# Turning activations to channels: f16 parts with tokens on the partitions, or f32 transposes with a split behind

## What is computed

```python
h = embed(x) * sqrt(192) + position
u = rmsnorm(layernorm(h)) * norm1_w
z, xBC, dt = split(u @ in_proj_w)            # 192 -> 384 + 512 + 24
y = scan(silu(conv4(xBC)), softplus(dt + bias)) * silu(z)
m = y @ out_proj_w
v = rmsnorm(m) * norm2_w
h = h + m + (silu(v @ w_gate) * (v @ w_up)) @ w_down   # MLP of 768
x = layernorm(h)
s = sigmoid(x @ gate_weight.T)               # 8 experts, 2 chosen of 2 groups of 4
out = h + shared_expert(x) + sum_of_chosen_experts(x)  # 9 pairs w1/w3 of 128, w2
```

## Time and profile before

| what | us |
|---|---|
| median of 3 runs | 852.89 (852.64 to 852.89) |
| the profiled execution | 854.33 |
| its span, first to last instruction | 852.5 |
| PE busy | 794.0 (93%) |
| DVE busy | 656.8 (77%) |
| ACT busy | 540.8 (63%) |
| POOL busy | 294.4 (35%) |
| mean granted PE clock | 0.986 of full speed |

### The profile page before, as it was taken

The page is one execution under the profiler, slowest core; times in us unless marked ns, Lnnn a source line. Parts: engine busy times, 40 slices in busy tenths (PEclk is TensorE's granted clock), DMA queues, the critical chain, the costliest instruction groups (busy, mean ns, idle before and its releaser), DMA issues.

```text
span 852.5 us, 23075 instructions
## 1 busy us (share of the span) xinstructions
PE 794.0 (93%) x7310; PEld 657.5 (77%) x7310; DVE 656.8 (77%) x1680; ACT 540.8 (63%) x1208; POOL 294.4 (35%) x445
## 2 busy tenths in 40 slices
PE   3567999999999999999999999999999999999897
PEld 2345787878888887888888787888878788887786
DVE  5785987977778797777879777787978778787645
ACT  4735576766667676666767676675767767576533
POOL 2552242343324234332423434242343424233222
PEclk9788999999999999999999999999999999999999
DMA  7600000000000000010000000000000000000000
GB/s 259 173 2 14 1 7 19 5 20 0 23 0 5 17 3 20 0 23 0 5 17 4 19 0 23 0 5 17 5 18 0 23 0 5 17 5 10 2 1 20
DMA packets 17107, 16.77 MB, mean 20 GB/s; under 512 B 6322, under 2 KB 15416, under 8 KB 16824
## 3 DMA queue, kind: packets, MB, share of 16 engines
q1 hardware_dynamic: 17080, 16.43, 6.8%
HBM read 12.23 MB, written 4.19 MB: 19 GB/s over the span
## 4 chain that ended last, share of the span: by engine, by line
PE 81%; DVE 6%; issue 5%; DMA 3%; ACT 3%; POOL 1%; SPq 1%; ACTq 0%; DVEq 0%; POOLq 0%
PE bank L1462 37%; PE bank L1743 7%; PE bank L1630 7%; PE bank L1812 6%; PE bank L1619 6%; PE bank L1712 4%; PE bank L1699 3%; PE bank L1690 3%; PE bank L1675 3%; DMA wt_raw<-weights 2%; DVE xa L1057 2%; PE bank L1468 2%; PE bank L1560 1%; PE bank L1470 1%; ACT L725 1%
## 5 line engine op out<-in xcount | busy, mean ns | idle before, releaser
L1114 DVE SCALAR_TENSOR_TENSOR mr<-er,gm 128x512 f32<-128x512 f32 x192 | 136.8, 735 | 29.1 <-ACT er L743 27.7
L743 ACT ACTIVATE er<-bank 128x512 f32<-128x512 f32 x192 | 109.5, 597 | 52.1 <-PE bank L1619 47.3
L1812 PE MATMUL bank<-w2t,w_raw 128*128 128x192 f32 x576 | 112.4, 326 | 0.0
L1057 DVE SCALAR_TENSOR_TENSOR xa<-xr,cw_,xa 128x256 f32<-128x256 f32 x192 | 92.9, 493 | 9.3 <-ACT xa L663 7.3
L814 ACT ACTIVATE sg<-bank 128x256 f32<-128x256 f32 x144 | 55.1, 383 | 59.3 <-PE bank L1462 48.2
L1812 PEld LDWEIGHTS bank<-w2t,w_raw 128*128 128x128 f32 x576 | 91.0, 190 | 1.3
L774 ACT ACTIVATE sg<-bank 128x256 f32<-128x256 f32 x90 | 34.6, 384 | 89.2 <-PE bank L1462 89.2
L1283 DVE TENSOR_TENSOR w_raw<-sg,bank 128x256 f32<-128x256 f32 x144 | 60.2, 418 | 37.3 <-ACT sg L814 36.1
L1462 PE MATMUL bank<-x_h,w_hi 128*128 128x256 f16 x288 | 78.3, 272 | 4.1 <-DVE w_raw L1283 3.9
L1630 PE MATMUL bank<-mr,xd 128*32 128x128 f32 x1536 | 69.4, 286 | 12.3 <-DVE mr L1114 12.1
L1462 PE MATMUL bank<-x_h,wt_lo 128*128 128x256 f16 x288 | 78.5, 273 | 0.0
(11 more groups left out here) (240 smaller groups left out, 2144.6 us busy)
## 6 DMA issues: line engine op xcount, KB each, us to landing
out<-w_raw SPq DMA_DIRECT2D x16, 192.0 KB, 2.0
w_raw<-weights SPq DMA_DIRECT2D x1, 1924.0 KB, 9.8
wt_raw<-weights SPq DMA_DIRECT2D x2, 962.0 KB, 15.6
pos<-position SPq DMA_DIRECT2D x16, 96.0 KB, 2.8
ri<-exponent_rows SPq DMA_DIRECT2D x4, 384.0 KB, 4.0
tok<-tokens SPq DMA_DIRECT2D x16, 70.0 KB
sums<-lj SPq DMA_DIRECT2D x16, 64.0 KB, 2.2
ri<-sums SPq DMA_DIRECT2D x64, 12.0 KB
```

Of the source, the lines that this page charges most:

```text
L743: act.activation(er[:, r % NER], p_d[r % 2][:].rearrange("p (h i) -> p h i", h=HG), ACT.Exp)\
L1057: ve.scalar_tensor_tensor(xa[:, m], xr[:, m, :, k:k + Q], cw_[:, m, k:k + 1], xa[:, m], ALU.mult, ALU.add)\
L1114: ve.scalar_tensor_tensor(mr[:, r % NER], er[:, r % NER], 1.0, gm[:, r // NQ, :].unsqueeze(1).to_broadcast([128, HG, Q]), ALU.min, ALU.mult)\
L1812: ins = pe.matmul(p_ex[e][:, b * D:(b + 1) * D], hh[:, e % NHH, b * Q:(b + 1) * Q], w2t[:, e, :], start=True, stop=True)
```

## The change

Each value is split while tokens are still on the partitions, and the f16 parts are turned.

- `u_t`, `v_t` and `x_t` hold for each channel the high and the low f16 part side by side (`[128, NB, D, 2]`). The high part: for u a new ACT step `pre_high` (two scalings of `uc`), for v `mixed_norm` with another destination, for x two DVE multiplications of `xc`. The low part: a new DVE step `low_parts`, two operations (source times scale minus high part).
- For u and x the mean is subtracted first, by two more DVE operations right behind the statistics (`uc`, `xc`).
- PE's `turn` does six f16 products with an f16 identity in place of four f32 transposes: two with the high parts of channels 0 to 127 (every second element of `u_t` as weights) after a wait for the high part; then, after a wait for the low part, two with both parts of channels 128 to 191 interleaved, and two with the low parts of channels 0 to 127, into another bank.
- Behind it ACT copies the bank to f16 in one operation of 512 elements (`high_in`), and DVE copies the low half in one of 256 (`low_in`).
- The tail's rows are now repeated one by one (c, c, c+1, c+1, ...) and not as a block; the host lays them out, and `wt_raw` comes in one DMA of 128 rows for each part.
- Order: v's turn moves behind the fifth `masked` and the eighth `exponents`; DVE's `v_low` stands between masks 4 and 5; `pre_low` stands behind the fourth gate product, ACT's `pre_high` behind the fourth `silu`; x's subtraction stands ahead of `steps_dt`, and its low part right behind its high part, ahead of masks 10 and 11. In the ramp `set_skip` moves behind the first split, an f16 identity is made by ACT, and DVE's weight split is in two steps.

The diff, cut to its core (ACT and the loads; then DVE; then PE and the host):

```diff
-                sp.dma_start(wt_raw[0:DT, part], weights[DH:D, part]).then_inc(in_w, 16)
-                sp.dma_start(wt_raw[DT:128, part], weights[DH:D, part]).then_inc(in_w, 16)
+                sp.dma_start(wt_raw[:, part], weights[DH:DH + 128, part]).then_inc(in_w, 16)
                 sp.dma_start(nrm[:], norms).then_inc(in_w, 16)
 
...
-            act.wait_ge(in_w, 64)
+            act.wait_ge(in_first, 48)
+            act.copy(id16[:], idf[:]).then_inc(setup_a, 1)
+            act.wait_ge(in_w, 48)
...
-            act.wait_ge(in_first, 48)
-            for k in range(KT):
-                act.activation(skip[:, k], idf[:], ACT.Copy, scale=dsk[:, k:k + 1]).then_inc(setup_a, 1)
-
-            def split(c, done, src, hi, taken, head, tail):
-
-                act.wait_ge(done, c + 1)
+
+            def set_skip():
+                for k in range(KT):
+                    act.activation(skip[:, k], idf[:], ACT.Copy, scale=dsk[:, k:k + 1]).then_inc(setup_a, 1)
+
+            def high_in(c, turned, src, hi, taken, ready):
+
+                act.wait_ge(turned, c + 1)
                 if later(c):
                     act.wait_ge(taken[0], c * taken[1])
-                act.copy(hi[:, 0, :], src[:, 0:NB * Q]).then_inc(head, 1)
-                act.copy(hi[DT:128, 1, :], src[DT:128, NB * Q:2 * NB * Q]).then_inc(tail, 1)
+                act.copy(hi[:], src[:].rearrange("p (k t) -> p k t", k=2)).then_inc(ready, 1)
 
...
             def mixed_norm(c, src=p_out[0]):
                 act.wait_ge(rm_ready, c + 1)
                 if later(c):
-                    act.wait_ge(vt_done, c)
+                    act.wait_ge(vl_turned, c)
                 for b in range(NB):
-                    ins = act.activation(vn[:, b, :], src[:, b * D:(b + 1) * D], ACT.Copy, scale=rm[:, b:b + 1])
-                ins.then_inc(vn_ready, 1)
+                    ins = act.activation(v_t[:, b, :, 0], src[:, b * D:(b + 1) * D], ACT.Copy, scale=rm[:, b:b + 1])
+                ins.then_inc(vh_ready, 1)
...
                     act.activation(sg[:, f % 2, :], p_pair[f % 2][:, 0:NB * Q], ACT.Silu).then_inc(sg_ready, 1)
+                    if f == 3 and p is not None:
+                        pre_high(p)
                     if f == 4 and p is not None:
                         pre_split(p)
...
+            def pre_high(c):
+                act.wait_ge(uc_ready, c + 1)
+                act.wait_ge(r0_ready, c + 1)
+                if later(c):
+                    act.wait_ge(ul_turned, c)
+                for b in range(NB):
+                    ins = act.activation(u_t[:, b, :, 0], uc[:, b, :], ACT.Copy, scale=r0[:, b:b + 1])
+                ins.then_inc(uh_ready, 1)
+
             def pre_split(c, src=p_misc):
-                split(c, ut_done, src, u_h, (z_done[0], 1), u_hi_ready, u_hi_tail)
+                high_in(c, uh_turned, src, u_h, (z_done[0], 1), u_hi_ready)
...
             def ramp():
+                pre_high(0)
                 pre_split(0)
+                set_skip()
                 softplus(0)
-                for i in range(2):
-                    convolved_in(0, i, p_d)
-                    first_tap(0, i)
+                convolved_in(0, 0, p_d)
+                first_tap(0, 0)
+                pre_high(1)
+                convolved_in(0, 1, p_d)
+                first_tap(0, 1)
                 gates(0, 1)
                 gates(0, 0)
                 pre_split(1, p_out[1])
```

```diff
-            def split(c, head, tail, src, hi, lo, lo_ready, lo_tail):
-
-
-                ve.wait_ge(head, c + 1)
-                ve.wait_ge(tail, c + 1)
-                ve.tensor_tensor(lo[:], src[:, 0:NB * Q], hi[:, 0, :], ALU.subtract).then_inc(lo_ready, 1)
-                ve.tensor_tensor(hi[0:DT, 1, :], src[DT:128, NB * Q:2 * NB * Q], hi[DT:128, 1, :], ALU.subtract)\
-                    .then_inc(lo_tail, 1)
+            def low_parts(c, src, scale, parts, ready):
+
+                for b in range(NB):
+                    ins = ve.scalar_tensor_tensor(parts[:, b, :, 1], src[b], scale[:, b:b + 1], parts[:, b, :, 0],
+                                                  ALU.mult, ALU.subtract)
+                ins.then_inc(ready, 1)
+
+            def low_in(c, turned, src, lo, ready):
+                ve.wait_ge(turned, c + 1)
+                ve.tensor_copy(lo[:], src).then_inc(ready, 1)
...
                 ve.wait_ge(h0_ready, c + 1)
+                if later(c):
+                    ve.wait_ge(uh_ready, c)
+                    ve.wait_ge(ul_ready, c)
...
                 ve.bn_aggr(mv[:, 1, :], stat[:, 1, :]).then_inc(stat_ready, 1)
-
-            def pre_apply(c):
+                ve.wait_ge(stat_ready, c + 1)
+                for b in range(NB):
+                    ins = ve.tensor_scalar(uc[:, b, :], h0_next[:, b, :], mv[:, b, 0:1], None, ALU.subtract)
+                ins.then_inc(uc_ready, 1)
+
+            def pre_low(c):
+                ve.wait_ge(uc_ready, c + 1)
                 ve.wait_ge(r0_ready, c + 1)
-                if later(c):
-                    ve.wait_ge(ut_done, c)
-                ve.tensor_scalar(un[:, 0, :], h0_next[:, 0, :], mv[:, 0, 0:1], r0[:, 0:1], ALU.subtract, ALU.mult)
-                ve.tensor_scalar(un[:, 1, :], h0_next[:, 1, :], mv[:, 1, 0:1], r0[:, 1:2], ALU.subtract, ALU.mult)\
-                    .then_inc(un_ready, 1)
-
-            def pre_split(c, src=p_misc):
-                split(c, u_hi_ready, u_hi_tail, src, u_h, u_l, u_lo_ready, u_lo_tail)
+                ve.wait_ge(uh_ready, c + 1)
+                low_parts(c, (uc[:, 0, :], uc[:, 1, :]), r0, u_t, ul_ready)
+
+            def pre_split(c, src=p_out[1][:, NB * Q:2 * NB * Q]):
+                low_in(c, ul_turned, src, u_l, u_lo_ready)
...
+                    if p is not None and t == 3:
+                        pre_low(p)
                     if f is not None and t in (0, 3):
                         masks(f, (6 + t // 3,))
                     if p is not None:
                         if t == 1:
                             pre_add(p)
                             pre_stats(p)
-                        if t == 2:
-                            pre_apply(p)
                         if t == 4:
                             pre_split(p)
...
                 ve.bn_aggr(mv2[:, 1, :], stat2[:, 1, :]).then_inc(stat2_ready, 1)
+                ve.wait_ge(stat2_ready, c + 1)
+                for b in range(NB):
+                    ins = ve.tensor_scalar(xc[:, b, :], h1[:, b, :], mv2[:, b, 0:1], None, ALU.subtract)
+                ins.then_inc(xc_ready, 1)
...
             def norm2_apply(c):
                 ve.wait_ge(r2_ready, c + 1)
-                if later(c):
-                    ve.wait_ge(xnt_done, c)
+                ve.wait_ge(xc_ready, c + 1)
+                if later(c):
+                    ve.wait_ge(xl_turned, c)
                 for b in range(NB):
-                    ins = ve.tensor_scalar(xn[:, b, :], h1[:, b, :], mv2[:, b, 0:1], r2[:, b:b + 1], ALU.subtract, ALU.mult)
-                ins.then_inc(xn_ready, 1)
+                    ins = ve.tensor_scalar(x_t[:, b, :, 0], xc[:, b, :], r2[:, b:b + 1], None, ALU.mult)
+                ins.then_inc(xh_ready, 1)
+                ve.wait_ge(xh_ready, c + 1)
+                low_parts(c, (xc[:, 0, :], xc[:, 1, :]), r2, x_t, xl_ready)
...
+            def v_low(c, src=p_out[0]):
+                ve.wait_ge(vh_ready, c + 1)
+                low_parts(c, (src[:, 0:D], src[:, D:2 * D]), rm, v_t, vl_ready)
+
             def split_v(b):
-                split(b, v_hi_ready, v_hi_tail, p_out[1], v_h, v_l, v_lo_ready, v_lo_tail)
+                low_in(b, vl_turned, p_pair[1][:, 0:NB * Q], v_l, v_lo_ready)
 
             def split_x(b):
-                split(b, x_hi_ready, x_hi_tail, p_out[1], x_h, x_l, x_lo_ready, x_lo_tail)
+                low_in(b, xl_turned, p_out[0][:, NB * Q:2 * NB * Q], x_l, x_lo_ready)
...
                 if f is not None:
                     masks(f, range(4))
                     from_state(f, 0)
-                    masks(f, (4, 5))
+                    masks(f, (4,))
+                v_low(b)
+                if f is not None:
+                    masks(f, (5,))
                 split_v(b)
                 mixed(b)
```

```diff
-            def transpose_channels(dst, src, done):
-
+            def turn(c, dst, low, parts, high_ready, low_ready, high_turned, low_turned):
+
+                pe.wait_ge(high_ready, c + 1)
                 for b in range(NB):
-                    pe.transpose(dst[:, b * Q:(b + 1) * Q], src[:, b, 0:DH], idf[:])
+                    pe.matmul(dst[:, b * Q:(b + 1) * Q], parts[:, b, 0:DH, 0], id16[:], start=True, stop=True)
+                pe.wait_ge(low_ready, c + 1)
                 for b in range(NB):
-                    ins = pe.transpose(dst[:, (NB + b) * Q:(NB + b + 1) * Q], src[:, b, D - 128:D], idf[:])
-                ins.then_inc(done, 1)
```

(37 more changed lines are left out.)

98 lines of the change are left out of this document (49 added, 49 removed).

## The result

The changed kernel takes 865.48 us (median of four runs, 864.00 to 866.65) against 852.76 before: a ratio of 1.0142, 95% interval 1.0122 to 1.0161. The forecast was 872.8. The profiled execution took 866.65 us with a span of 864.9.

What follows compares the result with a forecast made beforehand. TensorE, busy 93% of the span, was taken as the bound; 1.15 + 0.30 - 0.10 = 1.35 us per body, times 14 = 18.9, plus 1.0 finale, gave 19.9 and a median of 872.8 us, range 857 to 885.

Steps and rivals of the forecast that it cites:

- the waits ahead of the third product: Sign at x's and u's turns: TensorE idles until VectorE's low part, near 1.0 us per chunk for x with mask 9.
- masks 8 and 9 later: Sign on VectorE at x: masks 8 and 9 begin 0.7 us later behind the statistics.
- v's turn without its wait for ScalarE: Sign on TensorE: v's turn, now behind the fifth masked group, shows no wait for ScalarE's high part.
- x, 1.15 forecast: Term at x's turn: VectorE's added subtractions and low parts delay TensorE, costing 1.15 us per chunk.
- u, 0.30 forecast: Term at u's turn: ScalarE's high parts, then VectorE's low parts, cost 0.30 us per chunk, bounds 0.05 and 0.65.
- v, -0.10 forecast: Term at v's turn: a gain of 0.14 us per chunk, of which 0.10 was kept, bounds -0.2 and +0.2.
- The ramp, 0 forecast: Term before the loop: the wait for the wt_raw load covers the added operations, 0 us, bounds -1 and +1.
- The finale, +1.0 forecast: Term after the loop: chunk 14's v and x turns in the same surroundings cost +1.0 us, the last chunk's 0.
- Slow strided weights: Rival at the turns: products with stepped f16 weights take 0.11 us each, 4 to 6 us more, 878; chance 0.08.
- Low parts in time: Rival at x's and u's turns: low parts arrive without delaying TensorE, 0.7 us less per chunk, 843; chance 0.14.
- Absorbed: Rival behind the router: existing waits take up x's 1.15 us, 856, or 851.5 with u hidden too; chance 0.12.
- the rule weighed in the prediction: About 81 ns per weight load and 128-column matmul; two exposed turns in 14 chunks would cost 2.8 us more.

Runs made afterwards that it cites:

- u_high_vector: The changed kernel with u's high parts made by VectorE instead of ScalarE, one gate product earlier: 860.38 us, ratio 1.0070 to before.
- one_load: The kernel before with the doubled tail of the weights loaded by one transfer of 128 rows instead of two of 64: 848.21 us, ratio 0.9947.
- old_turns_later: one_load with its own f32 turns of u and x each issued one block of products later on TensorE: 859.81 us, ratio 1.0072 to before.
- v_only: one_load with v's new f16 turn in its new place, u and x turned as before: 845.88 us, ratio 0.9914 to before.
- x_old_u_later: The changed kernel with x turned as before (f32 transposes, split behind) and u's turn one block later: 844.45 us, ratio 0.9884 to before.
- both_later: The changed kernel with the turns of u and x each issued one block of products later on TensorE: 847.04 us, ratio 0.9908 to before.
- both_later_sub: both_later with x's pair of subtractions also moved behind masks 8 and 9 on VectorE: 848.45 us, ratio 0.9930 to before.

## Why the prediction was right, and where its terms were off

**The core held.** The loss is on VectorE ahead of the turns of x and u, and TensorE's f16 products save little. The places named in advance showed: the waits ahead of the third product, masks 8 and 9 later, v's turn without its wait for ScalarE, and a chunk of 50.8 where 50.9 was forecast. The profiled execution was forecast 19.9 us longer and came out 12.3 longer. Of the 7.6 between, 1.4 are in the loop, 4.9 in the ramp with the first body, and 1.2 in the finale. That the chunk was met within 0.1 us is in part luck: u came out 0.24 above its term, and x and v each some 0.2 below theirs.

**x, 1.15 forecast, 0.95 to 0.98 measured** (the latter as 1.23 less u's 0.54, plus v's 0.29). By the timeline: +0.39 in the masked group, start to start (505.68 to 506.72, against 500.05 to 500.70), and +0.56 in the turn with its wait (506.72 to 507.75, against 500.70 to 501.17). The term failed in two small prices. VectorE at x in the changed kernel, which answers to the earlier trace rows:

```profile
503.55 0.18 DVE L1215 BATCH_NORM_AGGREGATE mv<-stat 128x2 f32<-128x6 f32 x1 [0.16 <-DVE stat L1211]
503.68 0.18 DVE L1218 BATCH_NORM_AGGREGATE mv<-stat 128x2 f32<-128x6 f32 x1
503.90 0.55 DVE L1221 TENSOR_SCALAR xc<-h,mv 128x192 f32<-128x192 f32 x2
...
504.82 1.28 DVE L1141 SCALAR_TENSOR_TENSOR mr<-er,gm 128x512 f32<-128x512 f32 x2
506.02 0.56 DVE L1234 TENSOR_SCALAR x_t<-xc,r 128x192 f16<-128x192 f32 x2
506.62 0.76 DVE L1021 SCALAR_TENSOR_TENSOR x_t<-xc,r,x_t 128x192 f16<-128x192 f32 x2
507.29 1.29 DVE L1141 SCALAR_TENSOR_TENSOR mr<-er,gm 128x512 f32<-128x512 f32 x2
```

The pairs were right: 0.55, 0.56 and 0.76 against 0.54, 0.54 and 0.76. The two new waits of VectorE for its own last result were taken at 0.16 each, the value of the row between `bn_stats` and `bn_aggr`. They cost 0.04 (503.68 + 0.18 to 503.90, and 506.02 + 0.56 to 506.62). That is 0.24 too much; without it the working gives 0.93.

**u, 0.30 forecast, 0.54 measured.** From the end of the `silu` at 495.99 to the product behind the turn at 498.13 it is 2.14 us, where the working had 1.89 on the same footing. ScalarE's pair took 0.87 rather than 0.79 and began 0.07 behind the `silu`; the handover to VectorE took 0.14 (496.93 to 497.07) rather than 0.06. The four products, with what follows a wait, were right (497.90 to 498.13). The mis-sized term is the series over two engines, and u_high_vector shows that it holds nearly all that u costs.

**v, -0.10 forecast, -0.29 measured.** The working gave -0.14. Two small sizes make up the rest. I carried the 0.84 of the state products over from the chain, where a product that had waited stands behind them; without a wait the first swiglu product starts 0.75 us after them (488.71 to 489.46), which is 0.09 less. And mask 5 ends 2.17 us after the start of the high part (486.13 to 488.30) and not 2.23. In the kernel before, the same piece took 0.94 us (483.49 to 484.43). The 0.19 more was TensorE's wait for the old split of v, whose last operation on VectorE ends at 484.18; the one copy of the new turn ends in time.

**The ramp, 0 forecast, -3.6 with the first body measured.** This is the largest miss, and an edit costed at nothing. I let the transfer of `wt_raw` cover the added operations, and priced the new transfer itself at nothing. With two transfers the cover is real: the first product starts at 84.96 with the new turns and at 85.18 with the old. The one transfer takes the cover away. In the profiles it gives 7.3 us (85.2 to 77.9), and the changed kernel then starts 3.8 later (81.7). Neither number belongs to its edit alone: 1.5 us of each is TensorE's clock (last section), and 0.6 of the 3.8 is there before any turn. That leaves 5.8 us for the load and some 1.7 for the new turns. The first body, for which I had counted 1.35 like for any other, had no loss (52.19 against 52.27).

**The finale, +1.0 forecast, -0.2 measured.** I had counted it like a chunk of the loop. TensorE already waited 1.25 us for x's old split ahead of the router there (799.88) and waits 0.42 now (812.24), so that the shorter work behind the turn pays for the longer work ahead of it. The experiments hold v and x apart here (u is not turned in the finale). From its first swiglu product to the end it is 70.7 to 70.9 us with v and x both old (before, one_load, old_turns_later), 71.3 where v is new and x old (v_only, x_old_u_later), and 70.6 to 70.7 in the seven profiles where both are new: v's new turn costs about 0.5 us in the finale, and x's gives about 0.7.

**The rivals.** Slow strided weights fell with the first profile: a pair of products with stepped f16 weights takes 0.11 us (487.68 to 487.79, and 498.02 to 498.13), as much as the pair with contiguous ones between them (487.79 to 487.90), so 0.055 for one. "Low parts in time" is ruled out by the two waits. "Absorbed": none of x's delay came back behind the router, where the two kernels take the same 21.45 us to the next `project_out`.

By the rule weighed in the prediction (TensorE: Matmul & The Clock Gate, section "Back-to-back issue gap", of the Trainium skill) four of these products would take 0.32 us, an estimate worked out from that page; they take 0.23 (497.90 to 498.13).

## What to carry to other kernels

Where work is moved from behind a producer to ahead of it, look at the consumer's place in its queue too: here the change as made cost 1.23 us a chunk, and with both turns issued one block later the same operations cost nothing (49.48 against 49.57). Price the series from the last input to the low part and from the turn to its next reader separately, and put the turn where both fit; a part that then still costs (x, +0.35 a chunk in both_later: -0.09 less v's -0.29 and u's -0.15) is left as it was, and the parts that pay are kept (x_old_u_later, 0.9884). And when a load hides added work, ask whether the same change makes the load shorter.

## What the runs showed of the hardware

- VectorE's wait for its own result costs 0.04 us behind a `tensor_scalar` or `bn_aggr` and 0.16 behind `bn_stats`, in the same list (503.55, 503.90 and 506.62 above).
- Output with a step of two f16 elements costs VectorE nothing: the multiplication that writes it takes 0.56 us a pair, the f32 subtraction with contiguous output 0.55.
- TensorE's clock fell behind waits in the ramp. TensorE of the changed kernel was busy for 2.11 us of the stretch from 65 to 70 and waited 1.75 us for the sums until 71.45; from 70 to 75 its granted clock was 0.66 on average, partly the lower of its two levels (1.2 GHz, where 1.00 is 2.4). In one_load that wait ended at 69.13, and the clock was full from 70 on. Busy time by stretch (length, PE, PEld, DVE, ACT, POOL busy, granted clock, DMA share, GB/s), changed kernel and then one_load:

```profile
65.00:70.00 5.00, 2.11 (x16) 1.62 (x16) 4.08 (x7) 2.94 (x7) 1.47 (x2) 1.00 0.09 19
70.00:75.00 5.00, 3.55 (x12) 2.96 (x13) 1.29 (x2) 1.79 (x5) 0.16 (x1) 0.66 0.17 42
```

```profile
65.00:70.00 5.00, 3.57 (x17) 2.44 (x17) 1.92 (x4) 2.12 (x7) 1.63 (x2) 0.67 0.21 49
70.00:75.00 5.00, 5.00 (x58) 4.03 (x56) 3.50 (x6) 3.43 (x11) 0.91 (x2) 1.00 0.04 11
```

Six products of `project_out` took 2.13 us there and 1.14 in one_load. They take 2.13 in the kernel before as well, so this is no price of the new turns:

```profile
75.73 2.13 PE L1712 MATMUL bank<-wo,y 128*128 128x192 f32 x6
```

From the end of the wait for the sums to the first swiglu product it is 8.7 to 8.8 us in the three profiles whose clock was full by then (one_load, old_turns_later and, with new turns, both_later_sub) and 10.0 to 10.6 in the other eleven, 10.27 before and 10.24 in the changed kernel. So 1.5 us of one_load's 7.3 and of the 3.8 between it and the changed kernel are the clock. It also explains why both_later_sub has its first product at 78.6 and both_later at 81.1, though their ramps are the same code: 1.7 of the 2.5 us lie in this stretch. How often a kernel meets the full clock there stays open, since the profiles give one ramp for each kernel.
